# Perceiver block on one core: query, key and value weights split during the walk, the last two tiles in another order, three down products in three fp32r passes

## The reference

```python
k_prime = relu(einsum('bhnd,fd->bhnf', heads(ctx, Wk, bk), Wkf)) * mask   # 12544 rows, 16 heads x 64
kv      = einsum('bhnf,bhne->bhfe', k_prime, heads(ctx, Wv, bv))
k_sum   = sum(k_prime, axis=2)
x = x + (qkv / (q_prime . k_sum + 1e-8)) @ Wo.T + bo
z = layernorm(x)                          # second block, z1 = z
q, k, v = split(rms(z) @ w_qkv.T); w = exp(rms(k))
y = sigmoid(rms(q)) * cumsum(w * v) / (cumsum(w) + 1e-6)
u, g = split(y @ w_swiglu.T)
x = x + z + (u * silu(g)) @ w_out.T       # 2048 hidden, in 4 groups of 512
x = x + z + experts(z)                    # per expert 4 groups up, 4 groups down; top 1 by the router
```

## Time and profile before

| | us |
|---|---|
| median of 3 runs | 874.22 (874.15 to 874.38) |
| the profiled execution's own time | 874.06 |
| its span | 872.2 |
| PE busy | 862.2 |
| DVE, ACT, POOL busy | 668.4, 565.4, 363.3 |
| DMA | 64.15 MB |

### The profile page before, as it was taken

How to read it: one execution, slowest core, us unless ns; L and a number is a source line. 1 busy time by engine, 2 the same in 40 slices (tenths; PEclk the granted TensorE clock), 3 DMA queues, 4 the chain that set the end, 5 groups by cost and what they waited for, 6 DMA issues and landing times.

```text
span 872.2 us, 14770 instructions
## 1 busy us (share of the span) xinstructions
PE 862.2 (99%) x4726; PEld 742.5 (85%) x4726; DVE 668.4 (77%) x1050; ACT 565.4 (65%) x989; POOL 363.3 (42%) x208
## 2 busy tenths in 40 slices
PE   8999999999999999999999999999999999999998
PEld 7888888888888888888888888888888888778788
DVE  5777777777777777777777777777777778889586
ACT  5666666666666666666666666666666666674553
POOL 2654454445555445555544444555544433000000
PEclk9999999999999999999999999999999999999999
DMA  7212121121101010101010101101010000659740
GB/s 268 92 54 93 54 74 70 65 80 50 70 24 48 24 48 24 48 24 48 24 48 24 47 25 32 40 24 48 24 48 25 25 1 28 242 195 352 265 153 13
DMA packets 18505, 64.15 MB, mean 74 GB/s; under 512 B 2225, under 2 KB 2993, under 8 KB 18097
## 3 DMA queue, kind: packets, MB, share of 16 engines
q1 hardware_dynamic: 17760, 63.58, 20.7%
q10 hardware_dynamic: 720, 0.25, 0.1%
HBM read 63.56 MB, written 0.26 MB: 73 GB/s over the span
## 4 chain that ended last, share of the span: by engine, by line
PE 96%; DVE 2%; DMA 1%; issue 0%; ACT 0%; SPq 0%; DVEq 0%; ACTq 0%
PE kv_ps L799 11%; PE f_ps L786 10%; PE v_bank L702 10%; PE k_bank L702 10%; PE v_bank L703 10%; PE k_bank L703 10%; PE v_bank L704 10%; PE k_bank L704 10%; PE kv_ps L1026 3%; PE kv_ps L1045 2%; PE k_bank L882 1%; PE v_bank L882 1%; PE k_bank L888 1%; PE v_bank L894 1%; PE v_bank L888 1%; DMA early<-in_wk 1%
## 5 line engine op out<-in xcount | busy, mean ns | idle before, releaser
L413 POOL TENSOR_TENSOR ksum_acc<-ksum_acc,kf 128x1024 f32<-128x1024 f32 x96 | 231.0, 2406 | 189.9 <-DVE kf L1145 189.9
L501 ACT ACTIVATE fb<-f_ps 128x256 f32<-128x256 f32 x392 | 150.1, 383 | 171.4 <-PE f_ps L786 164.4
L1138 DVE TENSOR_TENSOR kf<-f_ps,fb 128x256 f32<-128x256 f32 x392 | 165.5, 423 | 108.4 <-ACT fb L501 103.1
L406 POOL TENSOR_TENSOR ctx_lo<-ctx_raw,ctx_hi 128x512 fp32r<-128x512 f32 x92 | 119.6, 1301 | 169.7 <-ACT ctx_hi L476 169.7
L786 PEld LDWEIGHTS f_ps<-bd,keys 128*128 128x128 f32 x784 | 146.3, 188 | 33.5 <-issue 1.3
L786 PE MATMUL f_ps<-bd,keys 128*128 128x256 f32 x784 | 155.9, 281 | 1.0 <-DVE kf L1138 0.9
L484 ACT ACTIVATE keys<-k_bank,bias_cols 64x512 fp32r<-64x512 f32 (+1 forms) x194 | 131.5, 678 | 34.3 <-PE k_bank L704 31.9
L702 PE MATMUL v_bank<-wv_hi,ctx_lo 128*128 128x512 f32 x388 | 153.2, 395 | 0.0
L702 PE MATMUL k_bank<-ctx_hi,wk_lo 128*128 128x512 f32 (+1 forms) x392 | 153.0, 390 | 0.0
L703 PE MATMUL v_bank<-wv_lo,ctx_hi 128*128 128x512 f32 x388 | 152.6, 393 | 0.0
L703 PE MATMUL k_bank<-ctx_lo,wk_hi 128*128 128x512 f32 (+1 forms) x392 | 152.2, 388 | 0.0
(11 more groups left out here) (218 smaller groups left out, 936.4 us busy)
## 6 DMA issues: line engine op xcount, KB each, us to landing
ctx_raw<-in_ctx SPq DMA_DIRECT2D x46, 512.0 KB, 3.2
early<-in_stream SPq DMA_DIRECT2D x14, 1024.0 KB, 4.8
raw<-in_stream SPq DMA_DIRECT2D x10, 1024.0 KB, 5.3
early<-in_stream SPq DMA_DIRECT2D x14, 512.0 KB, 4.3
early<-in_ctx SPq DMA_DIRECT2D x2, 512.0 KB, 6.3
early<-in_wv SPq DMA_DIRECT2D x1, 1024.0 KB, 8.6
early<-in_wq SPq DMA_DIRECT2D x1, 1024.0 KB, 10.4
w_o<-in_wo SPq DMA_DIRECT2D x1, 1024.0 KB, 5.1
```

The source lines that it names most:

```text
L406: pool.tensor_tensor(ctx_lo[:, s, :, cols], raw[:, :, t % 2 * P:(t % 2 + 1) * P], ctx_hi[:, s, :, cols].bitcast(f32), ALU.subtract).then_i ...
L413: pool.tensor_tensor(ksum_acc[:, :].rearrange("p (j f) -> p j f", f=P), ksum_acc[:, :].rearrange("p (j f) -> p j f", f=P), kf[:, t % 2, :, ...
L501: act.activation(fb[:, i % 2, :, :], f_ps[i % 2][:, :].rearrange("p (j x f) -> p j x f", j=2, x=2) [:, :, 1, :], ACT.Copy).then_inc(fb_rea ...
L1138: dve.tensor_tensor(kf[:, t % 2, 2 * i:2 * i + 2, :], f_ps[i % 2][:, :].rearrange("p (j x f) -> p j x f", j=2, x=2)[:, :, 0, :], fb[:, i % ...
```

## The change

Five edits:

1. The groups K, Q and V are split during the walk. Four groups (0 to 3) instead of seven are loaded early, into slots 3 to 6, since group g now lies in slot (g + 3) % 11. Their highs go to slots 0 to 2. In the three periods for chunks 19 to 21 ACT does one more copy per tile (`qkv_high`, 128x512, behind the keys) and DVE one more subtraction per tile (`qkv_low`, ahead of the first feature sum), twelve of each. The loop of ACT and DVE is two periods shorter, with these written out.
2. The down groups `GD[0]` to `GD[2]` join `SPLIT` and go through `hidden_down_split`, with `hidden_low` on DVE and `hid_hi` on ACT; `GD[3]` stays in plain fp32. The places of `weight_high` and `low_pieces` in the second block are new.
3. Tile 96's features are added to `ksum_acc` on POOL, so `feature_sums` has two parts instead of three, and both stand behind the key-values of tile 96.
4. In tile 97 the highs and lows of tile 96's features are done in two halves between the feature sums, and tile 97's mask in two halves as the sums come in.
5. The second block's `x + z` moves from DVE to POOL, to a place ahead of the gates; ACT and DVE wait for it.

```diff
-NG_EARLY = 7
+NG_EARLY = 4
+SLOTS_EARLY = 7
+BEFORE = [GK, GQ, GV]
+SPLIT = [GG[0], GU[0], GG[1], GU[1], GG[2], GD[0], GU[2], GG[3], GU[3], GD[1], GD[2], *GF_[0:6], GP[3],
...
+def slot_of(g):
+    return (g + 3) % RAWS
...
         def high(g):
-            return w_hi[SPLIT.index(g) % HIS]
+            return w_lo[g] if g in BEFORE else w_hi[SPLIT.index(g) % HIS]
...
             sp.wait_ge(f_done, JOBS * NT)
-            load_group(7)
-            load_group(8)
+            load_group(4)
+            load_group(5)
...
-            for g in range(RAWS, NG):
-                sp.wait_ge(group_used, g - RAWS + 1)
+            for g in range(8, NG):
+                sp.wait_ge(group_used, min(g - 7, 3) if g < 14 else g - 10)
                 load_group(g)
...
             pool.memset(ksum_k[:, :, :], 0.0).then_inc(kv_zero, 1)
+            add_features(NT - 2, 0)
...
+            z1 = gate[:, 0, :]
+            pool.wait_ge(act_ready, 4)
+            pool.tensor_scalar(z1, x1[:, :], stat[:, 6:7], stat[:, 8:9], ALU.subtract, ALU.mult).then_inc(z1_ready, 1)
+            pool.wait_ge(z1_ready, 1)
+            pool.tensor_tensor(x1[:, :], x1[:, :], z1, ALU.add).then_inc(x1_ready, 1)
...
+            def qkv_high(i):
+                g, k = BEFORE[i // KC], i % KC
+                act.activation(high(g)[:, k, :], raw(g)[:, k, :], ACT.Copy).then_inc(qkv_hi_ready, 1)
...
             def period_last(c, s):
                 n = TILES * c
                 for t in range(LAST_TILES):
                     values_last(n + t, s, t, [(c, s, n + t, t, i) for i in range(JOBS)])
-                    key_values(n + t - 1, t + 1)
+                    if t == 0:
+                        key_values(n - 1, 1)
+                pe.wait_ge(v_lo_ready, NT - 1)
                 for b in range(2):
-                    feature_sums(1, b)
+                    pe.wait_ge(kf_lo_ready, NT - 1 + b)
+                    for j in range(b * NPAIR // 2, (b + 1) * NPAIR // 2):
+                        last = key_value(j, 0, False, False)
+                last.then_inc(kv_done, 1)
+                pe.wait_ge(ksum_added, NT - 1)
+                for b in range(2):
+                    feature_sums(0, b)
                 for b in range(2):
                     pe.wait_ge(kf_ready, NT + b)
-                    last = feature_sums(2, b)
+                    last = feature_sums(1, b)
...
-                if n >= 3:
-                    hidden_down(n - 2, GD[n - 2], False, n == nd + 1)
+                if n in (3, 4):
+                    hidden_down_split(n - 2, GD[n - 2], False, False)
+            hidden_down(nd - 1, GD[nd - 1], False, True)
...
+            def tile_last(n, t):
+
+                features_sum(n, t, 0, False)
+                features_low_half(0, 0)
+                features_sum(n, t, 1, False)
+                features_low_half(0, 1)
+                masked_features_last(0)
+                for i in (2, 3):
+                    features_sum(n, t, i, False)
+                masked_features_last(1)
+                features_low_half(1, 0)
+                values_low(n, t, k_bank)
+                features_low_half(1, 1)
+
+            def qkv_low(i):
+                g, k = BEFORE[i // KC], i % KC
+                dve.wait_ge(qkv_hi_ready, i + 1)
+                dve.tensor_tensor(low(g)[:, k, :], raw(g)[:, k, :], high(g)[:, k, :].bitcast(f32), ALU.subtract)\
+                   .then_inc(qkv_lo_ready, 1)
...
+            before_gate = ((7, 10), (10, 13), (13, 16), (18, 20))
+            before_up = ((), (), (16, 18), (20, 21))
+            dve.wait_ge(x1_ready, 1)
             for n in range(nd):
+                low_pieces(*before_gate[n])
...
-                low_pieces(14 + 4 * n - 2 * (n == 3), 18 + 4 * n - 2 * (n >= 2))
-                if n == 2:
-
-                    dve.wait_ge(rstd_ready, 2)
-                    link(dve.tensor_scalar(eq[:, :], x1[:, :], stat[:, 6:7], stat[:, 8:9], ALU.subtract, ALU.mult))
-                    link(dve.tensor_tensor(x1[:, :], x1[:, :], eq[:, :], ALU.add))
+                if n:
+                    hidden_low(n - 1)
+            low_pieces(21, 26)
```

More of the change, by code:

```diff
@@ L66, in perceiver_kernel @@
         scope.close()
-        w_lo = [sb(f"w_lo{i}", [P, KC, D], f32r) for i in range(NG_EARLY)]
+        w_lo = [sb(f"w_lo{i}", [P, KC, D], f32r) for i in range(SLOTS_EARLY)]
         x_sb = sb("x_sb", [P, D])
@@ L807, in feature_sums @@
                     last = pe.matmul(v_bank[:, j * PAIR:(j + 1) * PAIR],
-                                     kf[:, part - 1, j, :] if part else ksum_acc[:, j * P:(j + 1) * P], ones[:, :],
-                                     start=part == 0 and j == 0, stop=part == LAST_TILES, skip_group_check=True)
+                                     kf[:, 1, j, :] if part else ksum_acc[:, j * P:(j + 1) * P], ones[:, :],
+                                     start=part == 0 and j == 0, stop=part == 1, skip_group_check=True)
                 return last
@@ L1045, in hidden_down_split @@
                                 last = pe.matmul(half_ps[b], x[n % 2][:, k, :], w[:, k, b * D // 2:(b + 1) * D // 2],
-                                                 start=False, stop=last_one and x is hid_lo and k == KC - 1)
+                                                 start=first and x is hid_hi and not low_w and k == 0,
+                                                 stop=last_one and x is hid_lo and k == KC - 1)
                     if bs == [0]:
@@ L1051, in _ @@
             nd = DFF // D
-            for n in range(nd + 2):
+            for n in range(nd + 1):
                 if n < nd:
@@ L1250, in _ @@
                 tile(t, t, first=t < 2, keys=((1, 1, t, k_bank, CHUNK),))
[L1251 removed]
+            with dve.Fori(1, LAST - 5, 2) as c:
                 period(c, 1)
                 period(c + 1, 0)
[L1254 removed]
+            period(LAST - 5, 1, pieces=1)
+            period(LAST - 4, 0, pieces=2)
+            period(LAST - 3, 1, pieces=3)
+            qkv_low(3 * KC - 1)
             period(LAST - 2, 0)
             period(LAST - 1, 1, keys=HALF)
[L1257 to L1266 removed]
+            tile_before_last(NT - 2, 0)
+            tile_last(NT - 1, 1)
+            low_pieces(0, 1)
             dve.wait_ge(kv_done, NT + 1)
@@ L1387, in _ @@
             turned(4)
+            low_pieces(26, 27)
             dve.wait_ge(logit_done, 1)
```

191 lines of the change are left out of this document (103 added, 88 removed).

## The result

| | before | changed kernel |
|---|---|---|
| median, us (8 runs each on the same chip) | 874.30 | 871.58 |
| ratio of times, 95% interval | | 0.9969 (0.9960 to 0.9979) |
| the profiled execution's own time | 874.06 | 871.90 |
| its span | 872.2 | 869.9 |

The changed kernel is faster by 0.31%. The forecast was 871.5, so the time and the sign came out. One run of the changed kernel at a granted clock of 0.65 (1214.49 us) is left out of the ratio; the median of the other seven is 871.55.

A forecast was written before the change was run, and what follows sets the result against it. PE, 96% of the chain that ends last, was taken as the bound. From 874.06 us, down products -1.8, sums -1.74 and tile 97's stall +0.9 gave 871.4, stated as 871.5 for the median; range 870.1 to 873.0.

The forecast's parts named there:

- The down products: Second block: three groups go from 3.45 to 2.83 us each on PE, a gain of 1.8 us (bounds 0.7 to 1.86).
- The sums: End of the walk: 32 feature-sum records remain, 16 fewer on PE at 0.109 us each, a gain of 1.74 us.
- The stall: Tile 97: PE's fourth feature job waits for DVE's half low, late behind POOL's add, costing 0.9 us (bounds 0 to 1.3).
- Rival A: Tile 97: POOL's add costs DVE nothing, so PE does not stall and the time is 870.6 us; chance 0.13.
- the lock: Tile 97: DVE's two-SBUF-input half low and POOL's add exclude each other, the later waiting for the whole; 0.9 us.
- The splits in the walk: Twelve walk tiles: added ACT copies and DVE `qkv_low` fit without delaying PE, cost 0 (bounds 0 to 1.4 us).
- x + z on POOL: Before the second block's gates: moved to POOL, x is there in time, cost 0 (bounds 0 to 1.0 us).
- DMA: Tail: three more groups, 3.1 MB, load in time at 352 GB/s full rate, cost 0, upper bound 3.0 us.
- Rival C: Tail: pieces of `GD[1]` or `GD[2]`, or x + z, come up to 1.1 us late, 872.6 us; chance 0.08.
- rival E: Walk: ACT waits for the early groups and the splits don't move, time as before, 874 us; chance 0.01.

The follow-up runs named there:

- e4: Changed kernel with the first three down groups back in plain fp32, without their highs, lows and hidden lows: 873.45 us, ratio 0.9991.
- e1: Changed kernel with tile 96's features summed on PE in a part of their own instead of added on POOL: 872.62 us, ratio 0.9981.
- e3: Changed kernel with POOL's add of tile 96 replaced by five memsets, tile 96 left out of the feature sum: 870.78 us, ratio 0.9961.
- e9: Changed kernel with POOL's add of tile 96 in halves, the second waiting for both half lows of tile 96 alone: 870.66 us, ratio 0.9961.
- e11: Changed kernel with POOL's two memsets released by tile 96's fourth feature share, so they run beside its mask on DVE: 872.22 us, ratio 0.9977.
- e5: Changed kernel without the twelve `qkv_low` subtractions in the walk, the high multiplied in place of the low: 871.62 us, ratio 0.9969.
- e6: Changed kernel with a second subtraction of the same size behind each of the twelve `qkv_low`: 879.40 us, ratio 1.0058.
- e8: Changed kernel with POOL's normalisation of x (128x512 TENSOR_SCALAR) done twice, one after the other, a single run: 872.75 us.
- e10: As e7, with POOL's two memsets behind tile 96's second half add instead of ahead of the first: 870.17 us, ratio 0.9954.
- e7: Changed kernel with tile 95's and 96's adds in halves, and tile 95's high, low and key-values in halves too: 870.87 us, ratio 0.9960.
- e2: Changed kernel with POOL's add of tile 96 in halves, the second waiting, by a miscount, for tile 97's first half low: 875.80 us, ratio 1.0014.

## Why the prediction was right, and where it was thin

**The down products: right.** Predicted -1.8; the stretch gave -1.85, and undoing the edit alone +1.87 (e4). The tightest piece has the cover that was reckoned: `GD[2]`'s last low (DVE, 804.80, 1.21 long) ends at 806.01, and PE asks for it at 807.59, 1.6 us later (1.7 predicted).

**The sums: right.** Predicted -1.74; e1 has 1.78 more in the chain.

**The stall: right, mechanism and size.** Predicted 0.9, a half low of about 1.9 us that ends 0.54 after the add; measured 0.83, 1.84 and 0.55. The difference is the release: 0.14 was taken, and the chain has 0.04 between the sum and the job. Four runs carry it: without POOL's add it goes (e1), with a POOL that only writes it goes (e3), with the add in halves it goes (e9, 0.92 us), with the add pushed later it grows (e11). Rival A, that the two share and nothing is lost, falls. Its time, 870.6, is the one that the kernel has once the lock is avoided: 870.66 in e9.

**The splits in the walk: right, on both sides.** Predicted `qkv_low` near 1.45 us and no gap: 1.44 and none. e5 shows the price 0. The margin was reckoned too thin: 0.03 us in one tile and 0.13 in most, against the 0.20 that e6 shows.

**x + z on POOL: term right, working wrong.** Its cost was 0 as predicted, but two of my numbers were not its own. I took the context low's 1.3 us for the TENSOR_SCALAR; it is 2.08 (e8). And I measured its cover to the first turn of `hid` at 788.63, while what it can collide with comes long before: two DVE products with both inputs in SBUF, 0.24 us behind its end. That these 0.24 us were there is luck, no part of the working. I had weighed what waits for the result and not what shares the port, although the same exclusion stood in the terms before. The bound of 1.0 us that I kept for it happens to be e8's price, for another reason.

**DMA: right, with a rate too low.** I took 352 GB/s for full DMA engines from 296 at 0.84; they carried 398 at 1.01. No PE gap followed. Rival C falls with PE's 35.90 busy us of 35.90, and rival E with the gain.

Not tried: edit 4 undone by itself, whether matmuls without use in e2's wait would have kept the clock, and which property of a POOL operation makes it hold a two-input one of DVE.

## What to carry to other kernels

Before moving work to POOL, look at what DVE does at that time: each operation with two SBUF inputs beside a two-input one of POOL, and each mask-like TENSOR_SCALAR even beside a memset, is a place where one engine waits for the whole of the other, and a wait that costs nothing where it arises is paid where the next one meets it. An operation that stands free in the queue is best placed by what runs beside it, not only by who needs its result: the add in halves around DVE's half lows gave 0.92 us (e9), and two memsets out of the mask's way 0.7 (e10 against e7). When an edit takes cover from PE, ask which engine's list is now the first to be late, and measure the margin by adding to that list: 0.03 us was reckoned, e6 showed 0.20, and 0.69 more on DVE cost 0.65 in each of twelve tiles.

## What the runs showed of the hardware

- DVE and POOL do not meet at semaphores alone, as was said at the start. A DVE operation that is held by POOL ends a fixed time behind it: 0.54 to 0.55 us (128x512 subtraction, 128x1024 mask), of 0.68 and 0.75 alone, and 0.28 (128x512 mask, 743.67 against 743.39 in e9), of 0.47 alone. POOL's context low, held by DVE, ends 1.15 behind it, of 1.33 alone.
- What POOL does counts: a two-input DVE operation runs freely beside memsets (0.69, e3) and beside POOL's TENSOR_SCALAR (0.42, e8), and is held by POOL's two-input operations. The mask is held by memsets too (1.32 and 1.16 instead of 0.75).
- A PE wait of 1.75 us inside dense work, with one of 0.92 seven us ahead of it and products of 64 columns behind it, was followed by a granted clock of 0.81 and then 0.50, and the median came out some 3 us above what the wait itself costs (872.5, against 875.8). Ten of e2's eleven executions lost clock, one (872.86) did not; without the wait (e9) none of five did. Two waits in the changed kernel (0.92 and 0.67 us by their brackets) and two in e11 (0.93 and 1.08) left the clock at 1.00.
- POOL's TENSOR_SCALAR with two per-row scalars (128x512, fp32) takes 2.08 us, more than its two-input TENSOR_TENSOR of that size (1.28); the ISA row ahead of its first use cost no time that the trace shows.
